# Attention: the low part of the probabilities of odd heads on POOL, that of even heads on DVE

## The reference

```python
q = (xn @ Wq.T).reshape(b, s, NUM_HEADS, HEAD_DIM)
...
attn = jnp.einsum('bqhd,bkhd->bhqk', q, k) * scale
causal = jnp.tril(jnp.ones((s, s), bool))
attn = jnp.where(causal[None, None], attn, -jnp.inf)
attn = jax.nn.softmax(attn, axis=-1)
h = jnp.einsum('bhqk,bkhd->bqhd', attn, v).reshape(b, s, hid)
x = residual + h @ Wo.T
```

## Time and profile before

| | |
|---|---|
| median of the runs | 2184.49 us (3 runs, 2183.06 to 2185.43) |
| span of the profiled execution | 2181.5 us |
| PE busy | 1906.3 us (87%) |
| DVE busy | 1211.0 us (56%) |
| ACT busy | 935.3 us (43%) |
| POOL busy | 376.7 us (17%) |
| first and last low part of the probabilities start at | 361.1 and 885.8 us |

### The profile page before, as it was taken

The page is one execution under the profiler, slowest core; times in us unless marked ns, Lnnn a source line. Parts: engine busy times, 40 slices in busy tenths (PEclk is TensorE's granted clock), DMA queues, the critical chain, the costliest instruction groups (busy, mean ns, idle before and its releaser), DMA issues. The chain is left out here.

```text
span 2181.5 us, 30371 instructions
## 1 busy us (share of the span) xinstructions
PE 1906.3 (87%) x10850; PEld 1633.6 (75%) x10850; DVE 1211.0 (56%) x1827; ACT 935.3 (43%) x1505; POOL 376.7 (17%) x391
## 2 busy tenths in 40 slices
PE   3878677899899899769999988999999999999980
PEld 2666455676676777658888868999999999999980
DVE  6886335726726636465555575555555555555544
ACT  4454333624525516422222215555555555555540
POOL 3233220010010100135000031111111111111115
PEclk9899886996987988889999998999999999999995
DMA  4664352260270261284020126555655555555527
GB/s 172 196 203 152 140 161 49 78 162 13 77 174 0 86 147 40 78 310 175 22 87 7 39 97 255 199 212 195 232 205 210 218 209 212 192 217 210 217 78 231
DMA packets 93795, 324.77 MB, mean 149 GB/s; under 512 B 8569, under 2 KB 25209, under 8 KB 75442
## 3 DMA queue, kind: packets, MB, share of 16 engines
q1 hardware_dynamic: 79122, 286.91, 38.7%
q0 software_dynamic: 6208, 20.98, 2.8%
q10 hardware_dynamic: 8416, 16.25, 1.9%
HBM read 232.47 MB, written 66.21 MB: 137 GB/s over the span
## 5 line engine op out<-in xcount | busy, mean ns | idle before, releaser
L46 PE MATMUL bank<-ex_x_hi,ex_w_hi 128*128 128x256 f32 x1472 | 419.4, 285 | 4.9 <-issue 4.9
L48 PE MATMUL bank<-ex_x_hi,ex_w_lo 128*128 128x256 f32 x1472 | 417.7, 284 | 0.0
L47 PE MATMUL bank<-ex_x_lo,ex_w_hi 128*128 128x256 f32 x1472 | 417.7, 284 | 0.0
L1148 DVE TENSOR_TENSOR ex_w_lo<-ex_stage,ex_w_hi 128x2048 fp32r<-128x2048 f32 x138 | 238.4, 1755 | 172.2 <-ACT ex_w_hi L1090 169.2
L46 PEld LDWEIGHTS bank<-ex_x_hi,ex_w_hi 128*128 128x128 f32 x1472 | 283.5, 193 | 7.9 <-issue 5.3
L47 PEld LDWEIGHTS bank<-ex_x_lo,ex_w_hi 128*128 128x128 f32 x1472 | 283.7, 193 | 2.7
L48 PEld LDWEIGHTS bank<-ex_x_hi,ex_w_lo 128*128 128x128 f32 x1472 | 283.5, 193 | 0.0
L1073 POOL TENSOR_TENSOR ex_a_lo<-ex_a,ex_a_hi 128x256 fp32r<-128x256 f32 x184 | 132.4, 742 | 679.1 <-ACT ex_a_hi L1110 679.1
L1105 ACT ACTIVATE ex_gate<-bank 128x256 f32<-128x256 f32 x184 | 70.5, 383 | 197.5 <-PE bank L48 197.5
L1926 PE MATMUL bank<-at_k,at_q 96*128 96x512 f32 (+3 forms) x256 | 115.2, 545 | 35.8 <-DMA at_k<-at_ones 24.5
L46 PE MATMUL bank<-ex_w_hi,ex_a_hi 128*128 128x512 f32 x368 | 144.3, 392 | 0.0
(11 more groups left out here) (254 smaller groups left out, 4338.9 us busy)
## 6 DMA issues: line engine op xcount, KB each, us to landing
ex_stage<-in_w_moe SPq DMA_DIRECT2D x69, 1536.0 KB, 6.3
first_w<-in_w_moe SPq DMA_DIRECT2D x23, 1536.0 KB, 6.5
scratch_tiles_in<-tm_zeros SPq DMA_DIRECT2D x4, 2944.0 KB, 17.3
scratch_tiles_out<-ex_y ACTq DMA_DIRECT2D x23, 512.0 KB, 3.3
at_q<-at_q_hi SPq DMA_DIRECT2D x32, 256.0 KB, 5.1
at_k<-at_k_hi SPq DMA_DIRECT2D x32, 256.0 KB, 6.4
cm_stage<-in_w_cm SPq DMA_DIRECT2D x8, 1024.0 KB, 8.2
first_x<-scratch_tiles_in SPq DMA_DIRECT2D x12, 512.0 KB, 6.9
```

The lines of the kernel that those rows point to most:

```text
L46: pe.matmul(out, lhsT=w_hi, rhs=x_hi, start=first, stop=False)
L47: pe.matmul(out, lhsT=w_hi, rhs=x_lo, start=False, stop=False)
L48: return pe.matmul(out, lhsT=w_lo, rhs=x_hi, start=False, stop=last)
L1148: return dve.tensor_tensor(dst, src, hi.bitcast(F32), ALU.subtract)
```

## The change

The low part of the probabilities of heads 1, 3, ..., 15 moves from DVE's queue to POOL's. Its semaphore is split in two, one for each engine, and the readers (PE for the output, ACT for the overwriting of `p_full`) wait for the one of the head's parity. POOL waits for the rounding itself, by ACT for heads 1 to 7 and by DVE for heads 9 to 15. On POOL's queue the eight subtractions of a pass stand behind the root for the next batch and ahead of `tail`.

```diff
-        p_lo_ready = sem("p_lo_ready")
+        p_lo_by_dve = sem("p_lo_by_dve")
+        p_lo_by_pool = sem("p_lo_by_pool")
...
+        def await_p_lo(engine, b, n):
+
+            engine.wait_ge((p_lo_by_dve, p_lo_by_pool)[n % 2], b * (HEADS // 2) + n // 2 + 1)
+
+        def await_p_hi(engine, b, n):
+
+            if high_by_dve(n):
+                engine.wait_ge(p_hi_by_dve, b * BY_DVE + rounded(n, True))
+            else:
+                engine.wait_ge(p_hi_by_act, b * (HEADS - BY_DVE) + rounded(n, False))
...
+            def low_probs(b):
+                for n in range(1, HEADS, 2):
+                    await_p_hi(pool, b, n)
+                    pool.tensor_tensor(p_lo1[:, :], p_full1[:, :], p_hi1[:, :].bitcast(F32),
+                                       ALU.subtract).then_inc(p_lo_by_pool, 1)
+
             with pool.Fori(0, B - 1) as b:
                 inverse_root(0, b + 1)
+                low_probs(b)
                 tail(b)
+            low_probs(B - 1)
             tail(B - 1)
...
                 if i >= 2:
-                    act.wait_ge(p_lo_ready, b * HEADS + i - 1)
+                    await_p_lo(act, b, i - 2)
...
                     dve.tensor_copy(p_hi[i % 2][:, :], p_full[i % 2][:, :]).then_inc(p_hi_by_dve, 1)
-                    dve.wait_ge(p_hi_by_dve, b * BY_DVE + rounded(i, True))
-                else:
-                    dve.wait_ge(p_hi_by_act, b * (HEADS - BY_DVE) + rounded(i, False))
-                dve.tensor_tensor(p_lo[i % 2][:, :], p_full[i % 2][:, :], p_hi[i % 2][:, :].bitcast(F32),
-                                  ALU.subtract).then_inc(p_lo_ready, 1)
+                if i % 2 == 0:
+                    await_p_hi(dve, b, i)
+                    dve.tensor_tensor(p_lo0[:, :], p_full0[:, :], p_hi0[:, :].bitcast(F32),
+                                      ALU.subtract).then_inc(p_lo_by_dve, 1)
...
-                pe.wait_ge(p_lo_ready, b * HEADS + n + 1)
+                await_p_lo(pe, b, n)
```

## The result

| | before | after |
|---|---|---|
| median of the runs | 2183.06 us (5 runs, 2180.64 to 2185.43) | 2192.39 us (5 runs, 2184.92 to 2193.78) |
| ratio | | 1.0035 (95% interval 1.0021 to 1.0049) |
| span of the profiled execution | 2181.5 us | 2183.3 us |
| DVE busy | 1211.0 us | 1171.9 us |
| POOL busy | 376.7 us | 468.9 us |

The changed kernel is slower, by 4.6 to 10.7 us. (The ratio comes from all the runs, not from the two medians, which lie 9.3 us apart.) The forecast was 2187.0 with a range of 2183 to 2194; the sign and the range hold, the size does not. 2192.39 lies outside the forecast case (2184.5 to 2188.9, chance 0.50) and inside what the first rival gave (2190 to 2198, chance 0.30). The profiled execution is the fastest of the five, and its span is only 1.8 us longer than before.

The account below looks back on a forecast made before the run. The prediction took PE and ACT to bound heads 0 to 7, and PE heads 8 to 15. It summed 2184.5 + 1.8 (0.45 lost per pass) + 0.7 (clock) = 2187.0 us, range 2183.0 to 2194.0.

Parts of the forecast that it names:

- forecast case: Whole kernel: the median lands between 2184.5 and 2188.9 us, predicted 2187.0; chance 0.50.
- first rival: Clock falls in PE's 2.1 us idle time before output 13: 4 to 12 us more, 2190 to 2198 us; chance 0.30.
- Heads 0 to 7: no gain: First half of a pass: odd low parts are off the critical path, so moving them to POOL saves 0.
- The ring: Heads 0 to 7: the cycle of dependent work repeating every two heads, claimed to stay at 8.81 us.
- Rival 4: Heads 0 to 7 gain because DVE was the limit: under 1 us per pass; chance 0.02, taken with another rival.
- POOL's price: Each low part moved to POOL, a 128x1280 subtraction, takes 2.89 us there, with bounds 2.82 and 3.17.
- The exclusion: DVE's subtractions and casts from SBUF and POOL's instructions lock each other out; whichever starts first keeps the other waiting.
- Rival 2: The lockout between DVE and POOL doesn't hold for these instructions: no loss, 2184.5 to 2185.5 us; chance 0.10.
- The drain: Last heads of a pass: PE waits for POOL before outputs 13 and 15; output 15 starts 2.9 us later.
- The way out gives most of it back: After the heads: the attention output's low part is no longer blocked by POOL, leaving 0.45 us loss per pass.
- The clock: PE's granted clock in its new idle stretches: 0.7 us added for one light fall in four passes.
- Rival 3: Shorter idle time before the projection keeps the clock at full, 1.6 us gained per pass: 2179.9 us; chance 0.08.

Follow-up runs that it names:

- h_first: Changed kernel with only heads 1, 3, 5 and 7 on POOL, all later heads on DVE: 2181.86 us, ratio 0.9993 to the kernel before.
- b_late: Kernel before, with POOL's addition to base held back until the low part of the attention output is done: 2176.03 us, ratio 0.9961.
- a_fill: Changed kernel plus eight unread products on PE before output 13 and eight before output 15: 2184.25 us, ratio 1.0006 to the kernel before.
- a_late: Changed kernel, with POOL's addition to base held back until the low part of the attention output is done: 2189.29 us, ratio 1.0020 to before.
- late_fill: Kernel before, with POOL's addition to base held back and fourteen unread products on PE ahead of the projection: 2166.57 us, ratio 0.9921.
- h_to11: Changed kernel with heads 13 and 15 back on DVE, odd heads 1 to 11 on POOL: 2183.29 us, ratio 1.0002 to the kernel before.
- h_second: Changed kernel with only heads 9, 11, 13 and 15 on POOL: 2188.98 us, ratio 1.0015 to the kernel before.
- b_fill: Kernel before, POOL's addition left where it was, with twenty-two unread products on PE ahead of the projection: 2179.31 us, ratio 0.9982.

## Why the prediction was right or wrong

- **Heads 0 to 7: no gain.** Right. The ring is 8.82 us, and h_first gives 0.9993 with 1 in its interval. Rival 4, a gain there, is out.
- **POOL's price.** Right: 2.94 against 2.89 us.
- **The exclusion.** Right, for both kinds of DVE instruction. The casts of heads 10, 12 and 14 end 0.68 to 0.69 us after POOL in every pass, and in b_late the 3127 ns go away with POOL's addition. The rule of the Trainium skill (page "SBUF — State Buffer", section "Who interferes with whom") is what the trace shows, 2906 ns for a cast of 828. I had expected the cast's end 0.85 after POOL, it was 0.69. Rival 2 is out.
- **The drain.** Right in its places. Output 13 at 419.64 (forecast 419.75), output 15 at 425.67 (425.85), cast 14 until 420.27, cast 15 at 421.81 (422.0). The ring of heads 8 to 12 is 6.09 us (POOL's low parts of heads 9 and 11 start at 402.22 and 408.31; forecast 6.14).
- **The way out gives most of it back.** Right in the mechanism: the low part of the attention output ends at 433.02, forecast 433.05. That the two agree to 0.03 us is partly luck. The prediction put the 3127 ns of rows 9 into the first pass, but they belong to the third; the first pass has 2979 ns, ending 0.55 us after POOL and not 0.70:

```profile
L1770 DVE TENSOR_TENSOR at_q<-at_o,at_q x4: 677/677/2979, 427.8 to 431.9; 128x512 fp32r<-128x512 f32 x4
```

  So the four take 2.49 us when nothing holds them out (4.79 - 2.98 + 0.68), not 2.34; 2.50 was measured. They also started 0.2 us earlier than forecast (430.52 against 430.7), and the two errors cancel. By the heads' times of passes without a fall, 72.02 against 71.45 us on average, the fixed loss is 0.57 us per pass and 2.3 in all, where the sum had 1.8; the whole profiles give about 3, a_fill's ratio 1.3 with an interval that reaches both. a_late against b_late shows the uncovered price, 2.6 us per pass.
- **The clock.** Here the sum failed. "I add 0.7 us, one light fall in four passes" stands against 7 falls in 16 passes of 1.35 us, 2.4 us per execution counted from profiles, and 4.4 us by the ratio of a_fill. The mechanism was named as rival 1, with its place (the idle time before output 13) and its price (1 to 3 us), and I gave it 0.30. The row it was judged by, a fall after about 2.2 us of idle time before the projection, spoke for it; the row against, 1.10 us without a fall, was only half as long as the new idle time and said little. The prediction had also named a fall inside the heads as a sign that it is wrong, and pass 3 of the changed kernel shows one at 732.8 us. The term should have been near two falls a run. With the 2.4 us of falls and the 2.3 us of the fixed loss the sum is 2184.5 + 2.3 + 2.4 = 2189.2, at the low end of the medians of the four kernels with this drain (2188.98 to 2192.39).
- **Rival 3**, a clock that stays up before the projection because PE idles less there, came in one pass of four. PE waits there 16.3 us in four passes instead of 25.6. PE's first product of the projection in passes 2 and 3:

```profile
590.34 0.77 PE L46 MATMUL bank<-at_q 128*128 128x512 f32 x1 [3.66 <-DVE at_q L1790]
...
748.09 0.47 PE L46 MATMUL bank<-at_q 128*128 128x512 f32 x1 [3.66 <-DVE at_q L1790]
```

  The idle time is 3.66 us in both. Behind it the granted clock is 0.50 in pass 2 (590.1 to 595.5, as in passes 1 and 4) and 1.00 in pass 3 (747.9 to 753.3), and the first addition comes after 5.71 and 3.50 us. Pass 3 is the one with the fall in the drain, so it got 2.2 us back that the heads' time does not show. The prediction's argument against this rival, that 3.3 us of idle time is more than the 2.2 us after which the clock fell, does not hold in pass 3. For the whole kernel the rival is still out: in the other three profiles with this drain the first addition never comes before 4.58 us. late_fill shows that the gain can be had in every pass, with work on PE to get it.

The 2.4 us counted as falls and the 4.4 us that a_fill takes away by the ratios don't meet fully. Profiles are few, so the rate of falls is loose, and what decides between a fall and none is not shown; I leave both open.

## What to carry to other kernels

An instruction moved to an engine that needs twice the time for it, and that keeps the first engine out meanwhile, relieved nobody here. It was harmless where a later step covers it (h_first, h_to11) and cost where the pipeline drains (h_second), so split by position in the loop, not by parity. Before moving work, look for the engine that already holds another one out at the end of the stage: here one wait on POOL (b_late) was worth more than any split. And count new idle time of PE twice, once as waiting and once as a chance that the granted clock falls behind it. A single profile that agrees with the sum proves little: here a gain in an untouched phase hid more than half of the loss.

## What the runs showed of the hardware that was not expected

- The granted clock fell to 0.50 behind idle times of PE of 1.96 us in some passes and not in others of the same kernel, 7 of 16, though that idle time was 1.93 to 2.05 us in all sixteen. It never fell behind the 1.1 us of the kernel before. Before the projection 3.66 us of idle time was followed by 0.50 in one pass and by 1.00 in the next.
- Such a fall cost 1.35 us from head 13 to the end of the way out; the output it hit took 3.3 us instead of 2.0.
- Products that nobody reads made the kernel faster by 0.4% beside the held-back addition (b_late 0.9961, late_fill 0.9921), and by 0.2% without it (b_fill 0.9982).
- A cast with one SBUF operand was held out by POOL as a subtraction with two is: it ended 0.68 us after POOL's instruction, the subtraction 0.55 us after. Row maxima read from PSUM were not: four of them took 1.68 us at 377.75, beside POOL's low part (377.34 to 380.28), and 1.68 us at 383.49 with POOL idle.
